# A transformer layer on one core: attention's values with the operands swapped, the four seams rewritten, and the FFN's chunks in groups of 4, 3, 2 and 2

## The reference

```python
def _L0_attn_ref(hidden_states, wq, bq, wk, bk, wv, bv, wl, bl):   # B, S, E = 4, 512, 512; H, D = 32, 16
    q = (hidden_states @ wq.T + bq).reshape(B, S, H, D)
    ...
    scores = jnp.einsum('bshd,bstd->bsht', q, k) / np.sqrt(D).astype(np.float32)
    probs = jax.nn.softmax(scores, axis=-1)
    context = jnp.einsum('bsht,bstd->bshd', probs, v).reshape(B, S, E)
...
def _L0_ffn_ref(x, w1, w2, w3):                                    # w1, w2: 1376 x 512, w3: 512 x 1376
    dq1 = nf4_quant_dequant(w1)
    ...
    h = jax.nn.silu(gate) * up
    return jnp.einsum('bsh,dh->bsd', h, dq3)
x = L0_attn_hidden_states
x = _layernorm(x + _L0_attn_ref(x, ...), axis=-1)
x = _layernorm(x + _L0_ffn_ref(x, ...), axis=-1)
```

## Time and profile before

| | |
|---|---|
| median of three runs | 812.72 us |
| the profiled execution, its span | 811.45 us, 809.6 us |
| PE, DVE, ACT busy | 737.6, 630.4, 484.5 us |
| projection, to the last L916 into `ps_p` of piece 47 | to 178.5 us |
| attention, to the FFN's first L914 | 178.5 to 393.1 us |
| FFN and output | 393.1 to 809.6 us |
| silu product L1295 on DVE, mean | 686 ns |

### The profile page before, as it was taken

One profiled execution on the slowest core, in us unless ns is written; L12 is line 12 of the kernel. 1 busy time (PEld: TensorE's weight loads), 2 busy tenths in 40 slices (PEclk: granted clock), 3 DMA queues, 4 the chain that ended last, 5 costly groups with the idle time before them and its releaser, 6 DMA issues.

```text
span 809.6 us, 14305 instructions
## 1 busy us (share of the span) xinstructions
PE 737.6 (91%) x5688; PEld 629.3 (78%) x5688; DVE 630.4 (78%) x876; ACT 484.5 (60%) x650; POOL 102.6 (13%) x97
## 2 busy tenths in 40 slices
PE   5899999765899999999699999997999999899993
PEld 4778788654899999999587888885888888688761
DVE  2799999579888898987488998877787575965286
ACT  3688989384654636556554778674674546663124
...
GB/s 221 232 159 156 148 155 157 257 243 259 234 214 189 226 262 135 278 157 133 232 1 203 85 210 26 81 54 26 141 30 171 45 4 35 118 148 12 104 157 155
DMA packets 89522, 118.45 MB, mean 146 GB/s; under 512 B 24784, under 2 KB 70864, under 8 KB 86512
## 3 DMA queue, kind: packets, MB, share of 16 engines
...
q10 hardware_dynamic: 1136, 2.10, 1.2%
...
## 4 chain that ended last, share of the span: by engine, by line
PE 63%; DVE 12%; issue 9%; ACT 6%; DMA 4%; SPq 3%; POOL 1%; POOLq 0%; DVEq 0%; ACTq 0%
PE ps_p L1013 9%; PE ps_s L914 9%; PE ps_s L916 9%; PE ps_s L915 9%; PE ps_p L914 7%; PE ps_p L916 6%; PE ps_p L915 6%; DVE nf_acc L1136 4%; ACT nf_y L747 3%; PE ps_s L1000 3%; DMA qk_parts<-qk_p 2%; PE ps_t L952 1%; PE ps_t L938 1%; DMA k_st<-qk_parts 1%; SPq L408 1%
## 5 line engine op out<-in xcount | busy, mean ns | idle before, releaser
L1136 DVE SCALAR_TENSOR_TENSOR nf_acc<-nf_y,nf_acc 128x1024 f32<-128x1024 f32 (+4 forms) x266 | 303.3, 1140 | 32.5 <-ACT nf_y L747 23.6
L747 ACT ACTIVATE nf_y<-nf_w,bound_b 128x1024 f32<-128x1024 f32 (+4 forms) x285 | 288.9, 1047 | 9.7 <-DVE nf_acc L1136 4.0
L1013 PE MATMUL ps_p<-probT,v_bd 128*68 128x32 f32 x1024 | 125.6, 301 | 3.3 <-DVE probT L1185 3.3
L1013 PEld LDWEIGHTS ps_p<-probT,v_bd 128*68 128x68 f32 x1024 | 122.9, 211 | 4.4 <-issue 3.2
L1295 DVE TENSOR_TENSOR silu<-silu,ps_s 128x512 f32<-128x512 f32 (+1 forms) x44 | 30.2, 686 | 91.4 <-PE ps_s L916 91.2
L914 PE MATMUL ps_p<-x_hl,w_hl 128*128 128x512 f32 x192 | 78.8, 410 | 16.0 <-DVE qk_r L1160 10.3
L891 ACT ACTIVATE silu<-ps_s 128x512 f32<-128x512 f32 (+1 forms) x44 | 26.2, 596 | 95.6 <-PE ps_s L916 95.6
L668 POOL TENSOR_TENSOR nf_w<-nf_w,nf_rec 128x1024 f32<-128x1024 f32 (+4 forms) x19 | 39.7, 2089 | 335.4 <-DVE nf_rec L1120 335.4
L914 PE MATMUL ps_s<-x_hl,f_ha 128*128 128x512 f32 x192 | 76.1, 396 | 5.7 <-issue 5.7
L916 PE MATMUL ps_p<-x_hl,w_hl 128*128 128x512 f32 x192 | 76.7, 399 | 0.0
L915 PE MATMUL ps_p<-x_hl,w_hl 128*128 128x512 f32 x192 | 76.5, 399 | 0.0
(11 more groups left out here) (105 smaller groups left out, 1246.6 us busy)
## 6 DMA issues: line engine op xcount, KB each, us to landing
...
```

Of the source, the lines that this page charges most:

```text
L747: act.activation(nf_y[0:p, at % NY, 0:w], nf_w[0:p, u % 2, 0:w], ACT.Identity, bias=bound_b[0:p, i:i + 1], scale=STEEP).then_inc(s_ny, 1)
L1013: t = pe.matmul(ps_p[0:MV, (G + 3) % NPV, i * H:(i + 1) * H], v_bd[hb % 2][:, :, g * GI + i], probT[:, G % 2, i], start=True, stop=True)
L1136: dve.scalar_tensor_tensor(out=acc, in0=y, scalar=float(NF4[i + 1]), in1=acc, op0=ALU.min, op1=ALU.max).then_inc(s_nacc, 1)
```

## The change

The first diff line changes the groups of chunks. In `values` the two operands change places: a token's 32 columns of `probT` are held, and the 68 columns of `v_bd` are moved, each token's output going to one of four strips of 32 partitions. The result has token and head on the partitions, so a new copy to `ctmp` (`evacuate`, ScalarE) and four transposes (`back`, TensorE) bring it to the old layout before `context`. The rest moves work at the seams: the loads of the first stacks, five levels, the turns between attention and the FFN, which now use two more banks, and the loads of `x1`.

```diff
@@ -62,7 +62,7 @@
...
-    GROUPS = [range(0, 4), range(4, 8), range(8, 10), range(10, NJ)]
+    GROUPS = [range(0, 4), range(4, 7), range(7, 9), range(9, NJ)]
...
-        UNITS += [("w", g, j) for j in js] + [("t", g, t) for t in range(2)]
+        first = len(js) if g == 0 else 1
+        UNITS += [("w", g, j) for j in js[:first]] + [("t", g, t) for t in range(2)] + [("w", g, j) for j in js[first:]]
...
+    def pairs(g):
+        js, out = list(GROUPS[g]), []
+        while js:
+            n = 2 if len(js) > 1 and rows_of(js[1]) == P else 1
+            out.append(js[:n])
+            js = js[n:]
+        return out
...
-        return [("f", u, s) for s in range(2 if kind == "w" else -(-len(GROUPS[g]) // 2))]
+        return [("f", u, s) for s in range(2 if kind == "w" else len(pairs(g)))]
...
-    NQK, NV, NPV = 5, 4, 4
+    NQK, NV, NCT = 5, 4, 3
...
+    FIRST_STACKS = [FIRST_LOAD + 1 + 2 * k for k in range(3)]
+    FIRST_VALUES = FIRST_LOAD + 7
     LV_P = [1, 1, 1, 1, 1, 1, 1, 1, 2, 2, 2, 2] * NBK
+    LV_P[-3:] = [1, 0, 0]
...
-        LV_A[8 * b + 10:8 * b + 13] = [1, 1, 1]
+        LV_A[8 * b + 11:8 * b + 14] = [1, 1, 1]
...
-    LV_F = [(1, 2)] * 2 + [(1, 1)] * 2 + [(1, 2)] + [(2, 2)] * (FIRST_OF[2] - 5) + [(3, 4)] * 4 + [(3, 3)] * 2
+    LV_F = [(1, 2)] * 2 + [(1, 1)] * 2 + [(1, 0), (1, 2)] + [(2, 3)] * 16 + [(3, 3)] * 12
...
-            CT_AT.setdefault(8 * b + 10 + k // 2, []).append(("ct", b, k))
-        MOMENTS_AT[8 * b + 12] = b
-        NORM_AT[8 * b + 13] = b
+            CT_AT.setdefault(8 * b + 11 + k // 2, []).append(("ct", b, k))
+        MOMENTS_AT[8 * b + 13] = b
+        NORM_AT[8 * b + 14] = b
         for c in range(KC):
-            XT_AT.setdefault(8 * b + 14 + c // 2, []).append(("xt", b, c))
...
-    LATE = {8 * b + 8 + k: 8 * b + 13 for b in range(NBK - 1) for k in range(2)}
...
+            XT_AT.setdefault(8 * b + 15 + c // 2, []).append(("xt", b, c))
...
+    LATE = {8 * b + 8 + k: 8 * b + 14 + k // 2 for b in range(NBK - 1) for k in range(4)}
...
-        CONTEXT_AT.setdefault(max(G + 3, LATE.get(G, 0)), []).append(G)
-    for G in range(GG):
+        CONTEXT_AT.setdefault(max(G + 4, LATE.get(G, 0)), []).append(G)
+        BACK_AT.setdefault(G + 4 if G % 8 == 2 and G > 8 else G + 3, []).append(G)
+    for G in range(GG + 1):
         TURNS += CT_AT.get(G, []) + XT_AT.get(G, [])
...
-    TAIL_1 = [("f", u, s) for u in T_UNITS for s in range(2)]
-    TAIL_2 = [("f", u, s) for u in W_UNITS[:2] for s in range(2)]
+    TAIL_1 = [("f", u, s) for u in (W_UNITS[0], T_UNITS[0]) for s in range(2)]
+    TAIL_2 = [("f", u, s) for u in (T_UNITS[1], W_UNITS[1]) for s in range(2)]
...
+    TAIL_S = (TAIL_1 + TAIL_2)[2:6]
+    def bank_of(n):
+        if n < NPT:
+            return n % 4
+        if TURNS[n] in TAIL_S:
+            return 2 + TAIL_S.index(TURNS[n]) % 2
+        return n % 2
+    EARLIER = {key: max((m for m in range(n) if bank_of(m) == bank_of(n)), default=-1) for key, n in TURN.items()}
...
+        def load_stacks(eng, hb, which=range(3)):
+            for b in which:
...
+            def load_x1(n):
+                b = ORDER[n][1]
+                if n == 0:
+                    sp.wait_ge(s_pv, GG - NG)
+                elif n == 1:
+                    sp.wait_ge(s_score, GG)
+                else:
+                    sp.wait_ge(s_up, LAST_STEP[max(k for k in range(n) if ORDER[k][1] == (b + 2) % NBK)] + 1)
+                x1_stored(sp, b)
+                sp.dma_start(x1_hl[b % 2][:].bitcast(F32), x1_d[b]).then_inc(s_ldx[b % 2], 16)
...
-                    load_stacks(sp, 0)
+                if tau in FIRST_STACKS:
+                    load_stacks(sp, 0, [FIRST_STACKS.index(tau)])
+                if tau == FIRST_VALUES:
                     values_stored(sp, KC)
                     sp.wait_ge(s_vzero[0], 2 * Q4)
...
+                if G == GG - 1:
+                    load_x1(0)
...
+            load_x1(1)
             levels(sum(LV_T))
-            load_x1(0)
-            load_x1(1)
...
+            def evacuate(G):
+                if G == 0:
+                    values_stored(act, KC * NBK)
+                act.wait_ge(s_pv, G + 1)
+                wait(act, s_back, G - NCT + 1)
+                act.activation(ctmp[:, G % NCT], ps_p[:, G % 2, 0:4 * MV], ACT.Copy).then_inc(s_evac, 1)
             def context(G):
                 hb, g = divmod(G, NG)
                 b, e = divmod(hb, 2)
-                act.wait_ge(s_pv, G + 1)
+                act.wait_ge(s_back, G + 1)
                 if e == 0 and g == 0 and b:
                     act.wait_ge(s_tr, TURN[("ct", b - 1, len(HEADS) - 1)] + 1)
                 at = TI * e + GI * g
                 act.activation(ctx[:, :, at:at + GI],
-                               ps_p[0:MV, (G + 3) % NPV].rearrange("p (i h) -> p h i", h=H), ACT.Copy
+                               ps_p[0:MV, 2 + G % 2].rearrange("p (i h) -> p h i", h=H), ACT.Copy
                                ).then_inc(s_ctx, 1)
...
                     context(at)
+                if G >= 3:
+                    evacuate(G - 3)
...
+            context(GG - 4)
+            evacuate(GG - 3)
+            for key in XT_AT.get(GG, []) + TAIL_1:
+                high(key)
+            evacuate(GG - 2)
             context(GG - 3)
-            for key in TAIL_1:
-                high(key)
-            context(GG - 2)
             steep(LV_T[0])
             for key in TAIL_2:
                 high(key)
-            context(GG - 1)
+            evacuate(GG - 1)
+            context(GG - 2)
             steep(LV_T[1])
...
+                if s == 0:
+                    context(GG - 1)
...
+                if EARLIER[key] >= 0:
+                    low_done(pe, TURNS[EARLIER[key]])
+                if key in TAIL_S[:2]:
+                    pe.wait_ge(s_ssub, GG)
...
-                wait(pe, s_ctx, G - NPV + 1)
+                wait(pe, s_evac, G - 1)
                 for i in range(GI):
-                    t = pe.matmul(ps_p[0:MV, (G + 3) % NPV, i * H:(i + 1) * H], v_bd[hb % 2][:, :, g * GI + i],
-                                  probT[:, G % 2, i], start=True, stop=True)
+                    a, j = divmod(i, 4)
+                    t = pe.matmul(ps_p[32 * j:32 * j + 32, G % 2, a * MV:(a + 1) * MV], probT[:, G % 2, i],
+                                  v_bd[hb % 2][:, :, g * GI + i], start=True, stop=True)
                 t.then_inc(s_pv, 1)
+            def back(G):
+                pe.wait_ge(s_evac, G + 1)
+                wait(pe, s_ctx, G - 1)
+                for a in range(4):
+                    t = pe.transpose(ps_p[0:MV, 2 + G % 2, P * a:P * a + P], ctmp[:, G % NCT, a * MV:(a + 1) * MV],
+                                     ident[:])
+                t.then_inc(s_back, 1)
...
-                        pe.wait_ge(s_ssub, GG)
+                        low_done(pe, TAIL_S[2 + w])
...
+                for at in BACK_AT.get(G, []):
+                    back(at)
...
-            for key in TAIL_1:
+            for key in XT_AT.get(GG, []) + TAIL_1:
                 turn(key)
+            back(GG - 3)
             values(GG - 1)
             for key in TAIL_2:
                 turn(key)
+            back(GG - 2)
...
+                if s == 0:
+                    back(GG - 1)
```

59 lines of the change are left out of this document (24 added, 35 removed).

## The result

The changed kernel takes 830.06 us (median of 4; 828.5 to 831.59) against 813.1 (median of 4) for the kernel before on the same chip: ratio 1.0208, 95% interval 1.0186 to 1.0229. It is slower, where 792.5 was forecast. Its profiled execution took 828.5 us, with a span of 826.7 and a mean granted clock of 0.921. One of the five executions of the later run f1 took 1620.85 us, twice the others, and counts in its median of 792.65 us (792.2 without it).

What follows compares the result with a forecast made beforehand. Attention was taken as bound by two equally long loops, TensorE's and VectorE's with ScalarE, the FFN by TensorE alone; 2 + 6 + 0.5 + 7.9 - 4.5 + 8.3 = 20.2 us gained gave 792.5 us, range 780 to 804.

Steps and rivals of the forecast that it cites:

- Attention's values: Attention: swapping the operands buys nothing by itself, since VectorE and ScalarE do the same work; blocks stay 47 to 49 us.
- V: TensorE's time for one attention group's values, put at 1.0 to 2.1 us; loops are equal at 2.0.
- Rival 1: Attention: strips do not run side by side, values take 4.2 us a group, 855 us, slower; 8 in 100.
- First seam: Before group 4: stores between thirds of the loads shorten waits, 6 us gained, bounds 0 and 13.
- The five levels: Before attention: five levels taken out, 1.2 us each on VectorE, lie in the DMA wait and buy nothing there.
- denser levels: FFN: earlier, denser VectorE levels make TensorE wait for drains, 4.5 us lost, bounds 0 and 9.
- Seam to the FFN: From group 31 to the first FFN matmul: 22.3 to 24.4 us, 0.5 gained, bounds -1 and 3.
- FFN groups: FFN group seams: two gaps of 5.0 and 2.9 us in TensorE's matmuls go, 7.9 us gained.
- width: Attention: unit 7, 832 wide instead of 1024, shortens ten levels by some 0.2 us each: 2 us gained.
- End: End of the FFN: two chunks per block leave 11.3 us beyond the matmuls instead of 19.6, 8.3 gained.

Runs made afterwards that it cites:

- f1: The changed kernel with four successive tokens in one strip and a group's x1_parts stores issued before its loads: 792.65 us, ratio 0.9739.
- h1: The kernel of f1 run again, on one chip beside h2 and h3: 795.38 us, ratio 0.9792.
- e1: The changed kernel with `values` in the form of the kernel before: 808.41 us, ratio 0.9934.
- e2: The changed kernel with each token's 68 moving elements side by side instead of 256 bytes apart, so other values are multiplied: 800.59 us, ratio 0.985.
- e3: The changed kernel with four successive tokens sent to the same strip, stride still 256 bytes: 803.47 us, ratio 0.9888.
- f2: The changed kernel with v_bd's second buffer padded, so odd head blocks read 272 bytes apart and even ones 256: 816.31 us, ratio 1.0035.
- h3: h1 with the five levels left before attention and four instead of six levels in the last two steps of the FFN's levels: 791.16 us, ratio 0.9737.
- h2: The kernel before with only the change's first seam and its FFN groups and levels: 794.08 us, ratio 0.9759.
- f4: e1 with a group's x1_parts stores issued before its loads: 800.19 us, ratio 0.9831.
- g4: The kernel before with only the FFN's chunks in groups of 4, 3, 2 and 2, and levels to match: 799.96 us, ratio 0.9843.
- j1: The changed kernel with tokens alternating between two strips, early x1_parts stores and the five levels left before attention: 789.07 us, ratio 0.9714.

## Why the prediction was wrong, point by point

- **Attention's values: the step that failed.** "So swapping the operands buys nothing here by itself: VectorE and ScalarE do the same work as before." They do the same work, but not in the same time. The working took V as a cost of TensorE alone and priced VectorE's loop by durations measured beside another pattern of reads. V itself came out at 2.0 us, inside the range, but with the clash in it, so that is luck: without the clash four strips take 1.0 to 1.26. Size of the miss: 34 us lost instead of 2.5 gained between group 4 and the FFN, a stretch of 221.4 us in the changed kernel and 184.1 in h1; e1, e2, e3 and, in its padded half, f2 each remove the slowing by another way. Rival 1 was on the right side with the wrong mechanism: the strips do run side by side (in e2 a recorded load and matmul of the values come every 0.031 us, though all of them take all 128 rows; that is far from this rival's 4.2 us a group), and that is the trouble.
- `back` took 0.60 to 1.07 us, not 1.95: it is four transposes, recorded as four instructions, not the eight that I priced. `evacuate` took 0.39 where nothing slowed it (0.50 on average in the changed kernel). Neither decided anything. Without the slowing (h1) a block is 49.1 us, as forecast (47 to 49), set by VectorE and ScalarE with TensorE idle a fifth of it. "Buys nothing" was nearly right once the slowing is gone: h3 is 2.9 us under h2, which is not clear of noise. With the turns moved in both, the new values in one strip are 5 to 8 us under the old ones (f1 and h1 against f4), since with the old values TensorE sets the pace of a plain group at 5.15 us, against 4.9.
- **A thing not priced: the moved turns.** The prediction counted the DMAs of the first seam and not those of group 15. The stores of x1_parts behind twelve loads cost 8 to 11 us as soon as the loop was fast (e3 to f1 and h1, e1 to f4).
- **First seam**, +6: right. 5.2 us alone; ScalarE's wait of 14.7 us for a part store fell to 1.9, piece 47 ended at 165.4, the second stacks came at 193.71 (forecast 195.7), group 4 at 197.18 (199.0), with the DMA engines full (a share of 1.03) from 170 to 194, as the argument had it.
- **The five levels**: "lie in this wait for DMA and buy nothing here" is right, and incomplete. They are not free where they go, the FFN: 4.2 us of the kernel's time (h3). The term **denser levels**, -4.5, was too small: in the changed kernel the FFN is 3.3 us longer than forecast (408.1 against 404.8). The waits for drains stand where I put them, at `down` of steps 22, 25 and 32, but are 2.2, 2.2 and 1.1 us instead of 1.4, 2.5 and 0.6; one more of 1.2 stands at step 8, and two waits for loads (2.6 in all) were not in the term. With the levels early the FFN takes 404.1 to 405.6 us (h3, g4, j1, h2).
- **Seam to the FFN**, +0.5: the seam takes 23.9 us in the changed kernel (0.2 gained) and 23.0 in h1, within the 22.3 to 24.4.
- **FFN groups**, +7.9: right; no wait for a chunk's split is left in the list of waits. With width and end, the groups alone gave 12.5 of 13.7 us.
- **End**, +8.3: right. TensorE is full from 748 to 808, its last matmul starts at 816.21, and the span ends at 826.7, 10.5 later; another us is lost between 808 and 816: 11.5 against 11.3 worked out.

With the two things that it had no price for taken out, the clash and the order of the stores, the kernel is where the forecast of 792.5 had it: f1 792.65, h1 795.38. The closeness of f1 is in part luck, since the same kernel was 2.7 us longer in h1, where the FFN took 4.5 us more than forecast and the stretch from group 4 to the FFN 1.5 less. The forecast of the kernel as written was 38 us off, and the range had no case in which another engine's instructions become longer.
